# A second set of feed-forward buffers, paired value products, halved adapter product and a new hand-written order in a four-layer gated block kernel

## The reference, cut to what matters

```python
x = x + tanh(g_xattn[0]) * matmul(fake_quant(layernorm(x)), fake_quant(ctx))       # layer 0 product, 8 bit
x = x + tanh(g_ffn[0]) * (h @ W_base.T + b + 0.5 * sum_e irfft((h @ enc.T) @ (coefs*mask)[e].T))   # h = layernorm(x)
x = x + tanh(g_xattn[1]) * attention(layernorm(x), ctx)      # 32 heads of 16, 8 key groups, mask, softmax in fp32
x = x + tanh(g_ffn[1]) * bitlinear(relu(bitlinear(h, w_gate))**2 * bitlinear(h, w_up), w_down)
```

## Time and profile before

| | us |
|---|---|
| median of 3 runs (lowest to highest) | 285.31 (283.99 to 285.43) |
| the profiled execution | 285.12 |
| its span, first to last instruction | 283.3 |
| TensorE busy in the span | 262.0 (92%) |
| VectorE, ScalarE, GpSimd busy | 211.9, 185.3, 115.4 |
| mean granted TensorE clock | 0.976 of full speed |

### The profile page before, as it was taken

The page is one execution under the profiler, slowest core; times in us unless marked ns, Lnnn a source line. Parts: engine busy times, 40 slices in busy tenths (PEclk is TensorE's granted clock), DMA queues, the critical chain, the costliest instruction groups (busy, mean ns, idle before and its releaser), DMA issues.

```text
span 283.3 us, 5004 instructions
## 1 busy us (share of the span) xinstructions
PE 262.0 (92%) x1617; PEld 128.4 (45%) x1640; DVE 211.9 (75%) x612; ACT 185.3 (65%) x311; POOL 115.4 (41%) x171
## 2 busy tenths in 40 slices
PE   8499899788899999999999999999999999899894
PEld 8326358545443343374244275324244253256581
DVE  3777956668887399886969962989988555969682
ACT  3602389568488989786589785888598577452232
POOL 3003304826311055575556475769646556100000
PEclk9879799999799999999999999999999999999999
DMA  6999945150592800057600000800001000000000
GB/s 182 410 409 417 373 191 111 38 102 21 132 364 81 141 0 2 1 194 281 102 0 3 0 2 3 156 9 1 5 0 39 0 0 3 0 37 2 37 2 37
DMA packets 7665, 27.56 MB, mean 97 GB/s; under 512 B 1344, under 2 KB 3952, under 8 KB 5880
## 3 DMA queue, kind: packets, MB, share of 16 engines
q1 hardware_dynamic: 7208, 21.55, 25.8%
q0 software_dynamic: 288, 5.70, 5.2%
q10 hardware_dynamic: 144, 0.00, 0.0%
HBM read 23.79 MB, written 3.41 MB: 96 GB/s over the span
## 4 chain that ended last, share of the span: by engine, by line
PE 73%; DVE 10%; ACT 10%; issue 5%; DMA 1%; POOL 0%; DVEq 0%; ACTq 0%
PE bank L760 10%; PE bank L787 10%; PE bank L738 10%; PE bank L671 5%; PE bank L681 5%; PE bank L828 5%; PE bank L763 4%; PE bank L810 4%; PE bank L847 3%; PE bank L746 3%; PE bank L706 2%; ACT big L968 2%; PE bank L613 2%; PE bank L622 2%; PE bank L716 2%
## 5 line engine op out<-in xcount | busy, mean ns | idle before, releaser
L1194 DVE CUSTOM_DVE_ANT_0 junk<-bank,maskb 128x512 bf16<-128x512 f32 x128 | 83.9, 687 | 19.7 <-PE bank L738 18.9
L968 ACT ACTIVATE big<-bank 128x512 f32<-128x512 f32 x128 | 74.5, 596 | 27.1 <-PE bank L760 11.6
L549 POOL TENSOR_TENSOR big<-big,product 128x512 int32<-128x512 int32 x48 | 61.6, 1284 | 49.6 <-ACT big L968 49.2
L738 PE MATMUL bank<-kst,qst 96*128 96x512 bf16 x128 | 48.9, 386 | 2.4 <-DVE mx L1194 1.6
L760 PE MATMUL bank<-qst,kst 99*128 99x512 bf16 x128 | 49.5, 386 | 0.9 <-ACT qst L951 0.5
L787 PE MATMUL bank<-big,vp 128*32 128x512 f32 x256 | 33.7, 604 | 1.5 <-POOL big L549 0.5
L738 PEld LDWEIGHTS bank<-kst,qst 96*128 96x128 bf16 x128 | 12.6, 99 | 33.9 <-issue 24.9
L763 PE MATMUL bank<-ident_b,maskb 128*128 128x512 bf16 x65 | 24.7, 380 | 0.0
L951 ACT ACTIVATE qst<-bank 3x512 bf16<-3x512 f32 x32 | 18.9, 590 | 7.0 <-PE bank L746 6.4
L760 PEld LDWEIGHTS bank<-qst,kst 99*128 99x128 bf16 x128 | 12.5, 98 | 21.8 <-ACT big L968 6.6
L828 PE MATMUL bank<-ternary,hqT 128*128 128x512 bf16 (+1 forms) x95 | 20.7, 356 | 1.2 <-ACT hqT L985 1.0
(11 more groups left out here) (167 smaller groups left out, 403.2 us busy)
## 6 DMA issues: line engine op xcount, KB each, us to landing
stage_w<-in_w_down POOLq DMA_DIRECT2D x1, 2816.0 KB, 11.5
stage_w<-in_w_gate SPq DMA_DIRECT2D x1, 2752.0 KB, 21.7
stage_w<-in_w_up POOLq DMA_DIRECT2D x1, 2752.0 KB, 12.1
qst<-q_parts SPq DMA_DIRECT2D x18, 128.0 KB, 4.9
big<-in_ctxT SPq DMA_DIRECT2D x2, 1024.0 KB, 15.5
q_parts<-parts SPq DMA_DIRECT2D x12, 128.0 KB
x<-in_x SPq DMA_DIRECT2D x4, 256.0 KB, 14.2
big<-in_ctx SPq DMA_DIRECT2D x4, 256.0 KB, 5.0
```

Of the source, the lines that this page charges most:

```text
L549: nc.gpsimd.tensor_tensor(p, p, keep[:, nt, KEEP_ST.index(i):KEEP_ST.index(i) + 1, :].broadcast_to([P, HG, P]), ALU.mult).then_inc(kept, 1)
L738: mm(o[:, :], qst[0:KS, tile % 2, g * HG + hh, :], kst[0:KS, tb(tile)[0], g, :], start=True, stop=True).then_inc(fill(stage), 1)
L968: fn(pt[:, c % 4, s, :], o[:, :], ACT.Exp).then_inc(drain(stage), 1)
L1194: v.tensor_tensor_reduce(junk[:, j % 2, :], o[:, :], maskb[:, tb(c // NG)[1], :], 1.0, HIDE, ALU.add, ALU.max, mx[:, c % 3, 0, hh:hh + 1]) ...
```

## The change

1. A second set of feed-forward buffers: tiles 1 and 3 use `gate`, `hid_q` and `hid_qT` in `stage_w` and an `hqT` in `hT`. The waits that named tile t-1 name t-2; tile 1 waits for all ternary pieces (12) and for the last query product first. The output factor gets a column for each tile.
2. The products with the values are issued in pairs, at the second and fourth of the four steps.
3. The adapters' product: each of the four blocks of the sum is a product of 64 columns (40 used), blocks 0 and 2 to the lower half of the partitions, 1 and 3 to the upper, in one bank. The encoders are loaded twice, at partitions 0 and 64, into a cleared buffer, and the product with them sums 128 partitions.
4. The factors for the context's quantisation are signalled apart (`scales_ready`), before tanh; the rest is a stage `products`.
5. `psum_uses` keeps a use that starts before the first score and ends after it off the score banks.
6. New order of the free stages in `PREPARATION` and `FILL`.

```diff
@@ schedule
-        if i >= 0 and i % 16 < 4 and i // 16 < NSC:
-            s.append(("pv", i // 16, i % 16))
+        if i >= 0 and i % 16 in (1, 3) and i // 16 < NSC:
+            s += [("pv", i // 16, i % 16 - 1), ("pv", i // 16, i % 16)]
@@ psum_uses
+    late = list(range(S_BANKS, 8))
...
+        drained_at = at[drain_stage(use)]
+        if now < at[("s", 0)] < drained_at:
+            banks = late if drained_at < at[("t", 0, 0)] else late[T_BANKS:]
@@ buffers
-        gate = hid[:, 0:FF]
+        gates = (hid[:, 0:FF], stage_w[:, 0:FF])
-        hid_q = hid[:, FF:FF + FT * P // 2].bitcast(BF16)
+        hid_qs = (hid[:, FF:FF + FT * P // 2].bitcast(BF16), stage_w[:, FF:FF + FT * P // 2].bitcast(BF16))
+        hqTs = (hqT, hT[:, 0:KT // 2, :].rearrange("p a n -> p (a n)").bitcast(BF16).rearrange("p (k n) -> p k n", k=KT))
-        hid_qT = sb("hid_qT", [P, FT, P], BF16)
+        hid_qTs = (sb("hid_qT", [P, FT, P], BF16)[:, :, :],
+                   stage_w[:, FF + FT * P // 2:FF + FT * P].bitcast(BF16).rearrange("p (k n) -> p k n", k=FT))
-        enc = early[0:RR, 0:D]
-        vt_sb = early[0:RR, D:2 * D]
+        enc = early[:, 0:D]
+        vt_sb = early[:, D:2 * D]
@@ SP
-            sp.dma_start(enc, enc_in).then_inc(ld_enc, 16)
+            sp.wait_ge(enc_cleared, 1)
+            for half in range(2):
+                sp.dma_start(enc[64 * half:64 * half + RR, :], enc_in).then_inc(ld_enc, 16)
@@ TensorE, vt
-                    for k in range(KT):
-                        i = mm(o[0:RR, :], coef[:, k, 0, :], dft[:, k, :], start=(k == 0), stop=(k == KT - 1))
+                    for k in range(0, KT, 2):
+                        for half in range(2):
+                            i = mm(o[64 * half:64 * (half + 1), :], coef_rows[:, k + half, 0:64], dft[:, k + half, :], start=(k == 0),
+                                   stop=(k == KT - 2))
@@ ScalarE
-                    act.wait_ge(scalars_ready, 1)
+                    act.wait_ge(scales_ready, 1)
...
-                    wait_filled(act, ("u", t - 1, 2) if t else ("p", NT - 1))
-                    fn(hqT[:, :, :], o.rearrange("p (k n) -> p k n", k=KT), ACT.Copy).then_inc(drain(stage), 1)
+                    wait_filled(act, (("p", NT - 1), ("q", NT - 1))[t] if t < 2 else ("u", t - 2, 2))
+                    fn(hqTs[t % 2][:, :, :], o.rearrange("p (k n) -> p k n", k=KT), ACT.Copy).then_inc(drain(stage), 1)
...
-                    if t and stage[2] == 0:
-                        act.wait_ge(hid_q_ready, 2 * t)
+                    gate = gates[t % 2]
+                    if t == 1 and stage[2] == 0:
+                        act.wait_ge(ternary_ready, 12)
+                    if t > 1 and stage[2] == 0:
+                        act.wait_ge(hid_q_ready, 2 * (t - 1))
...
-                    if t:
-                        wait_filled(act, ("y2", t - 1))
+                    if t > 1:
+                        wait_filled(act, ("y2", t - 2))
@@ VectorE, fq
-                        if t and k == 2:
-                            wait_filled(dve, ("f2T", t - 1, 1))
+                        if t > 1 and k == 2:
+                            wait_filled(dve, ("f2T", t - 2, 1))
```

More of the change, by code:

```diff
@@ L122 @@
-    101: [("ffactors", 0)], 103: [("fternary", 2, 2), ("gu", 0, 2, 1)],
[24 rows of a table removed]
+    2: [("fternary", 0, 2), ("v", 1, 3), ("fternary", 0, 3), ("hT", 1, 2)], 4: [("fload", 1)],
[6 rows of a table added]
+    32: [("fscale", 1), ("fround", 1, 0)], 33: [("fclamp", 1, 0)], 34: [("oT", 0), ("fround", 1, 1)],
+    35: [("ln2", 2, 5)], 38: [("hT", 2, 2)], 39: [("keepT",)],
+    41: [("ln1", 3, 0), ("fround", 1, 2), ("fclamp", 1, 1), ("fternary", 1, 0), ("fround", 1, 3)],
[16 rows of a table added]
+    105: [("ffactors", 0), ("ln3", 1, 5)], 106: [("fround", 2, 3)], 108: [("hidden", 0, 1), ("ln3", 1, 6)],
@@ L147 @@
+    110: [("gu", 0, 2, 1)], 111: [("fclamp", 2, 1)], 117: [("hidden", 0, 2)], 118: [("aT", 2, 0)], 119: [("oT", 5)],
+    120: [("fq", 0, 0)], 121: [("fclamp", 2, 2), ("fternary", 2, 0)],
+    122: [("ffactors", 1), ("fclamp", 2, 3), ("fternary", 2, 1)], 123: [("fternary", 2, 2), ("fternary", 2, 3)],
[22 rows of a table added]
 }
@@ L318, in gated_blocks_kernel @@
         cst = sb("cst", [P, 16], F32)
-        RS1, RS2, ZC1, ZC2, ALPHA, NAZ1, NAZ2, KZZ, WPROD, WDT = range(10)
+        RS1, RS2, ZC1, ZC2, ALPHA, NAZ1, NAZ2, KZZ, WPROD, WDT, WOUT = range(11)
         rowt = sb("rowt", [P, 1], F32)
@@ L827, in _ @@
                     for k in range(KT):
-                        i = mm(o[:, 0:n], hqT[:, k, :], tern[w][:, k * FF + c0:k * FF + c0 + n], start=(k == 0),
+                        i = mm(o[:, 0:n], hqTs[t % 2][:, k, :], tern[w][:, k * FF + c0:k * FF + c0 + n], start=(k == 0),
                                stop=(k == KT - 1))
@@ L846, in _ @@
                     for k in range(k0, k1):
-                        i = mm(o[:, :], hid_qT[:, k, :], tern[2][:, k * D:(k + 1) * D], start=(k == 0), stop=(k == FT - 1))
+                        i = mm(o[:, :], hid_qTs[t % 2][:, k, :], tern[2][:, k * D:(k + 1) * D], start=(k == 0), stop=(k == FT - 1))
                     if stage[2] == 2:
@@ L896, in _ @@
                     o = wait_filled(act, stage)
-                    fn(vt_sb[:, :], o[0:RR, :], ACT.Copy).then_inc(drain(stage), 1)
+                    fn(vt_sb[:, :], o[:, :], ACT.Copy).then_inc(drain(stage), 1)
                 elif kind == "q1T":
@@ L1001, in _ @@
                     o = wait_filled(act, stage)[:, 0:(k1 - k0) * P // 2].bitcast(BF16)
[L1002 to L1004 removed]
+                    if t > 1:
+                        wait_filled(act, ("y2", t - 2))
+                    fn(hid_qTs[t % 2][:, k0:k1, :], o.rearrange("p (k n) -> p k n", n=P), ACT.Copy).then_inc(drain(stage), 1)
         @block.vector
@@ L1059, in before @@
                 return s[-1] if s else None
-            link("hidden", v.memset(hid_q[:, FF:FT * P], 0.0))
+            link("hidden", v.memset(hid_qs[0][:, FF:FT * P], 0.0))
             after("hidden")
@@ L1067, in _ @@
                     dve.wait_ge(ld_scal, 16)
-                    link("constants", v.reciprocal(cst[:, RS1:RS2 + 1], scr[:, 4:6]))
-                    after("constants")
+                    v.reciprocal(cst[:, RS1:RS2 + 1], scr[:, 4:6]).then_inc(scales_ready, 1)
+                elif kind == "products":
                     link("constants", v.tensor_scalar(cst[:, ZC1:ZC2 + 1], scr[:, 6:8], -128.0, None, ALU.add))
@@ L1263, in _ @@
                     f = fs[:, t % 2]
+                    gate, hid_q = gates[t % 2], hid_qs[t % 2]
+                    if t == 1 and k == 0:
+                        dve.wait_ge(ternary_ready, 12)
+                        link("hidden", v.memset(hid_q[:, FF:FT * P], 0.0))
                     if k == 0:
@@ L1288, in _ @@
                             after("weights")
-                            link("out", v.tensor_scalar(f[:, 5:6], f[:, 10:11], cst[:, WDT:WDT + 1], 1.0 / 127.0, ALU.mult, ALU.mult))
+                            link("out", v.tensor_scalar(cst[:, WOUT + t:WOUT + t + 1], f[:, 10:11], cst[:, WDT:WDT + 1], 1.0 / 127.0, ALU.mult, ALU.mult))
                 elif kind == "y2up":
@@ L1292, in _ @@
                     after("out")
-                    v.scalar_tensor_tensor(out=x[:, t, :], in0=o[:, :], scalar=fs[:, t % 2, 5:6], in1=x[:, t, :],
+                    v.scalar_tensor_tensor(out=x[:, t, :], in0=o[:, :], scalar=cst[:, WOUT + t:WOUT + t + 1], in1=x[:, t, :],
                                            op0=ALU.mult, op1=ALU.add).then_inc(drain(("y2", t)), 1)
```

27 lines of the change are left out of this document (10 added, 17 removed), and 113 rows, old and new, of tables (FILL, PREPARATION).

## The result

| | median us (lowest to highest) | ratio to before, 95% interval |
|---|---|---|
| before, beside it | 284.65 (282.66 to 285.43) | |
| after | 273.34 (273.01 to 274.45) | 0.962 [0.9559, 0.9681] |

The profiled execution of after took 273.56 us, 11.56 less than that of before.

A forecast was written before the change was run, and what follows sets the result against it. TensorE's list was taken to bound the attention (busy 173.8 of 179.8 us). The terms -3.5 - 5.9 + 0.8 + 0.8 + 1.5 + 0.3 = -6.0 took 285.12 to 279.1 us; range 275.0 to 284.3.

The forecast's parts named there:

- rival E: Start of the attention: the 1.22 us gap and the half-clock stretch after it go, 276.2 us; chance 0.14.
- part 3: Attention: 1.55 us of work enters where TensorE partly stands still, half charged, +0.8 us.
- part 4: Attention, steps 121 to 124: three ternary pieces in a burst on ScalarE hold up TensorE, +0.8 us.
- part 2: Attention: feed-forward work of tiles 0 and 1 moves behind it, off TensorE's list, -5.9 us.
- Part 1: Attention: value products in pairs give 15 fewer separate runs at 0.235 us each, -3.5 us.
- rival B: Attention: pairing gains nothing, as the second group's weights load only behind the first's products; 282.6 us, chance 0.09.
- Part 6: Preparation: first score product 0.3 us later; nothing of the adapters' product reaches the path, because of the wkv wait.
- Part 5: After the attention: moved work added, 0.4 us of waits allowed, 37.2 instead of 35.7 us, +1.5.
- C: Last part: VectorE's 32.8 us and small waits bound it, 35.7 + 5; 282.6 us in all, chance 0.15.
- D: Attention: ScalarE and the two exponential banks bound it, TensorE's savings become waits; 287.7 us, chance 0.09.
- F: Second buffer set fails its purpose, the order keeps tiles apart, small waits eat the rest; 284 to 285.5 us, chance 0.10.
- other signs: Trace marks, among them: last value product 7 to 9 us earlier than 244.4, first context product still at 21 us.

The follow-up runs named there:

- pair_only: The kernel before with the products with the values issued in pairs and nothing else changed; 282.19 us, ratio 0.9907.
- old_order: The kernel after with all its new code but the old order of free stages everywhere; 281.75 us, ratio 0.9913.
- late_new: The kernel after with the old order of free stages up to step 51 and the new one from step 52 on; 274.72 us, ratio 0.9654.
- early_new: The kernel after with the new order of free stages up to step 51 and the old one behind it; 280.63 us, ratio 0.9867.
- joined: The kernel after with all four groups of value products of a round in one step instead of pairs; 280.49 us.
- lone_late: The kernel after with one group of value products a step, each a step later than in lone_values; 277.66 us.
- lone_values: The kernel after with one group of value products per step, as before, instead of pairs; 280.97 us.
- no_fill: The kernel after without the two runs of 74 fill products behind the attention; 272.87 us, ratio 0.9597.
- fill_20: The kernel after without the first run of 74 fill products and with 20 in the second; 272.14 us, ratio 0.9569.

## Why the prediction was off

The sign and most mechanisms were right; the size was not: -11.6 us in the profiled executions against -6.0. Point by point, with what each step had and what the profiles show:

| step | predicted | measured | from |
|---|---|---|---|
| 1 pairs | -3.5 | -2.8 | attention of before to pair_only, -4.4, less 1.7 for the half-clock stretch; medians of the whole kernels: -2.7 |
| half-clock stretch | 0 (rival E) | -1.7 | steps 0 to 24, before to pair_only |
| 2 and 4, late order and burst | -5.9 + 0.8 | -8.2 | attention of old_order to late_new |
| 3 entering work | +0.8 | +0.1 | attention of old_order to early_new |
| 5 last part | +1.5 | +1.4 | 35.70 to 37.08 |
| 6 preparation | +0.3 | -0.4 | first score product; it lies between 63.85 and 66.13 with the old preparation, and between 63.74 and 64.19 in five kernels with the new one |

**The step that failed is the treatment of waits in the attention, parts 3 and 4.** Both set a charge on work that falls beside other work, +0.8 each. In part 3 that work filled gaps and cost nothing. In part 4 the burst cost no wait: the last 100.7 us of after's attention hold 0.1 us of idle time in TensorE, in spite of the ternary pieces at 209.10 and 211.70 us. Steps 121 to 124 take TensorE 6.5 us (207.93 to 214.44), as the sum had it; but ScalarE's surplus of 0.8 us does not stop TensorE. ScalarE then works without a gap past 217 us, and no product waits for it. The first piece and the copy of the row maxima (done at 211.2) fit under a pair (209.53 to 211.46), as in the place shown beside joined. And the prediction did not ask what the moved work did to the waits that were there. In old_order TensorE is idle for 2.8 us in the last 109 us of the attention, in late_new for 0.9 of 101:

```profile
132.20:241.55 109.35, 106.52 (x633) 44.76 (x643) 87.06 (x256) 82.59 (x144) 68.95 (x86) 1.00 0.12 24
```

```profile
130.85:231.53 100.68, 99.74 (x592) 40.97 (x602) 81.77 (x247) 79.28 (x138) 68.46 (x86) 1.00 0.12 22
```

Ten or eleven mask products lack records in each of these stretches, which makes some 0.8 us of either figure. By the listed waits it is 1.8 us in old_order and none in late_new, so the fall of 1.9 stands.

Part 4 with the right sign would have read -1.9 instead of +0.8, part 3 zero: 3.5 of the 5.6 us of the miss. About 0.45 more is part 2's price of the moved work (6.35 for 5.9); the half-clock stretch (1.7) and the preparation (0.7), less the pairs (0.7), make up the rest.

**Part 1** was right in its mechanism and 0.7 us too large in the old order, where TensorE's listed waits rise by 0.4 us with it (3.9 to 4.3). In the new order the same pairing is worth 4.3 (lone_late) to 7.6 us (lone_values), the larger figure since it also moves groups behind GpSimd. A pair takes 1.92 us against twice 1.06. By the Trainium skill's rule on weight loads ("TensorE: Matmul & The Clock Gate", Part 3) pairing would be worth nothing, rival B; for these products the measurement decides against it.

**Part 6** was right where it said that nothing of the adapters' product reaches the path, for the reason that it gave. **Part 5** was right in size, and its waits even less than allowed: none.

**Rivals.** C (VectorE bounds the last part) did not happen: VectorE is busy 30.07 of 37.08 us, where the prediction had 32.8. It is near, though; without fill products TensorE waits for it, 2.9 us earlier than now. D (ScalarE and the banks) did not happen either; joined, with 9.3 us of listed waits, is the nearest to it. F was true of the buffers in the old order and wrong of the change. E happened: in after both the gap of 1.22 us and the stretch at half clock are gone, and the stretch was worth 1.7 us. The gap alone does not bring it, since the profiles of pair_only, old_order and late_new have the gap and not the stretch. But a clock as low as in before's profile is in most runs of before and in none of 40 with the new early order. So by the clocks that profile was the usual case of before, and the sum, which put the end of the stretch at nothing, left out a gain of the change and not a chance of one run.

Of the other signs that the prediction named, the last value product comes 13.0 us earlier and not 7 to 9, and the first context product starts at 19.93 instead of 21 us, behind an idle time of 0.47. The prediction also read before's 6.0 us of idle time in the attention as it stands; 15 missing records are in it.

**Open.** The medians give the early order 1.1 to 1.4 us (old_order to early_new, late_new to after), though the attention shows 0.1. Among runs at 0.986 or more the two steps are 280.96 to 280.31 (one run) and 273.53 to 273.56 (one run), so most of it goes with the clock; in which stretch is not shown, since the other runs have no profile. The burst was not spread out in a run of its own; that it costs nothing is read from the trace.

## What to carry to other kernels

When work leaves a nearly full engine, look at the waits that this work caused, too, and give them a sign of their own; a charge "to be safe" on every moved piece adds up to an error on one side. When work enters where the engine has idle time of the same size, its first price is zero. Before subtracting from a single profile, hold its granted clock against those of the other runs: is its half clock the usual case, or this run's own? Count the records of an operation against the source before reading idle time as waits. A stretch of products that needs nothing from another engine is the place to put under it what that engine must get done. And size fill products by the wait that they cover, by taking them out once.

## What the runs showed of the hardware

- A group of eight fp32 products on 32-column tiles costs 0.85 us in a row and 0.21 to 0.235 more for each separate run of groups: 0.235 by the starts of the earlier trace rows, 0.22 from lone_late against after, 0.21 from before to pair_only (4.44 us, less 1.67 for the half clock, and 0.4 more of listed waits, over 15).
- Two products of 64 columns on the two halves of the columns start 0.01 us apart and run side by side: eight take four slots. One after the other they take eight.
- The same idle gap of 1.2 us was followed by a stretch at half clock in the profile of before and by none in those of pair_only, old_order and late_new. A wait of 2.78 us without fill products before it was followed by half clock in no_fill, one of 1.46 us behind 20 fill products by none in fill_20.
- A trace can lack records of matmuls, here 14 to 16 of 80 products of one kind in nine of fourteen traces, while their weight loads are all there. That reads as up to 1.6 us of idle time in 180.
